# Cross-attention stage on one core: where two TensorE steps stand in the order of a unit

## The chip, the cores and the metric

The kernel runs on one core of one Trainium2 chip. A core has TensorE (PE), VectorE (DVE), ScalarE (ACT), GpSimd (POOL) and SyncE (SP, which only issues transfers here). Each engine takes its instructions in the order of its own program and they meet through semaphores. The metric is the device time of one execution in microseconds (us).

## The reference

The reference is a stack of four layers over x (4, 256, 512), each a gated cross-attention on a context (4, 64, 512) and a gated feed-forward part:

```python
x = x + jnp.tanh(g_xattn[3]) * _L3_xattn_ref(_layernorm(x, axis=-1), ctx_4096, mask, L3 weights ...)
x = x + jnp.tanh(g_ffn[3]) * _L3_ffn_ref(_layernorm(x, axis=-1), L3 ffn weights ...)
```

The change lies in the fourth cross-attention. It has 32 query heads and 8 key and value heads of width 128, an RMS norm over each query head and key head, a softmax over 64 keys, and an output projection:

```python
q = (hidden_states @ q_proj_w.T).reshape(B, Q, 32, 128).transpose(0, 2, 1, 3)
k = (cross_attention_states @ k_proj_w.T).reshape(B, KV, 8, 128).transpose(0, 2, 1, 3)
v = (cross_attention_states @ v_proj_w.T).reshape(B, KV, 8, 128).transpose(0, 2, 1, 3)
q = rmsnorm(q, q_norm_w); k = rmsnorm(jnp.repeat(k, 4, axis=1), k_norm_w); v = jnp.repeat(v, 4, axis=1)
scores = jnp.einsum('bhqd,bhkd->bhqk', q, k) * scale + attention_mask
attn = jax.nn.softmax(scores, axis=-1)
out = jnp.einsum('bhqk,bhkd->bhqd', attn, v)
return out.transpose(0, 2, 1, 3).reshape(B, Q, 4096) @ o_proj_w.T
```

## The kernel before

The program is written engine by engine; every engine's order is the order of its Python function, and waits are written by hand as semaphore counts. The fourth attention consists of `pe_x3`, `act_x3`, `dve_x3`, `pool_x3` and `sp_x3`.

It is cut into `NU0` = 32 units, u = 4 g + b. Group g (0 to 7) is one key head with its four query heads, b (0 to 3) one batch entry of 256 rows (two tiles, tt = 0 and 1). Products that need full precision are made of three (`mm3`, lines 150 to 152) from a high and a low half of each operand: ScalarE writes the high half, VectorE or POOL the rest.

The parts of a unit on TensorE:

- `queries(u, tt)`: twelve products of 512 columns, into bank tt.
- `turn_q(u, tt)`: four transposes of the queries (line 963) into bank 2.
- `scores(u)`: keys `kT` as weights against the turned queries (line 972) into bank 2. The scores come out with keys on the partitions, so ScalarE copies them to `S_TURNED` (line 1130) and `turn_s(u)` turns them back with four transposes (line 982) into bank 3.
- On VectorE `shift(u)` scales bank 3 by the queries' norm (line 1238), adds the mask (line 1242), takes the maximum (line 347) and subtracts it (line 349). ScalarE's `exps(u)` and VectorE's `norm(u)` finish the softmax.
- `turn_p(u)`: four transposes of the probabilities (line 991) into bank 4. ScalarE's `probs_t(u)` writes the high half, VectorE's `probs_low(u)` (line 1253) the low one.
- `outputs(u, tt)`: six products (lines 150 to 152) into bank 5 + tt, which VectorE's `add(u, tt)` adds to X (line 1265).

The output projection is folded into the values ahead of time, eight products a group: `fold_outputs` (line 940) into bank 7, copied by ScalarE's `folded_high` (line 1106) and subtracted by VectorE's `folded_low` (line 1258). `folds(u, slot)` says which fold stands in which of three slots of a unit. For b = 0 and 1 these are slots 1 and 2, for b = 2 slot 2 alone, for b = 3 all three; the later folds of a group are made at b = 0 and 1, the first ones of the next group at b = 2 and 3.

Once a group `keys_values(g)` makes keys and values: sixteen products of line 917 and eight of line 921, all into bank 7. ScalarE copies them (lines 1092 to 1096), VectorE squares and sums the keys (`key_squares`), POOL makes the scale (`key_scale`), VectorE applies it (`key_norm`, line 1222), and `turn_k(g)` (line 928) turns the keys on TensorE at b = 2, behind `turn_q(u + 2, 1)`. Bank 7 is one chain of ten pieces a group (`piece(r)`): each waits until ScalarE, and for a fold VectorE too, is through with the piece before.

The units are pipelined by two. The loop over u on TensorE runs: `queries(u + 2, 0)`, `turn_p(u)`, the fold of slot 0, `queries(u + 2, 1)`, `turn_q(u + 2, 0)`, the fold of slot 1, `outputs(u, 0)`, `turn_q(u + 2, 1)`, `turn_k(g + 1)` if b = 2, `outputs(u, 1)`, `scores(u + 2)`, the fold of slot 2, `turn_s(u + 2)`, and `keys_values(g + 1)` if b = 1. VectorE's loop runs: `shift(u + 1)`, `probs_low(u)`, `key_squares` if b = 2, the low half of the fold of slot 0, the sums of squares, `norm(u + 1)`, `key_norm` if b = 2, the low half of slot 1, `add(u, 0)`, `add(u, 1)`, the low half of slot 2, and in the last group row statistics (line 1346). The split weights of the next group's queries come from ScalarE (`high_q`) and POOL (`split_q`) at b = 0 and 1, two chunks of four at a time.

Of the kernel before, what the change touches and what calls it, by code (L numbers as in the profile page):

```python
# [18 lines left out]
NG, HG, DH = 8, 4, 128  # L19
# [38 lines left out]
def build(nc, x_d, ctxT_d, ctxB_d, gx_d, gf_d, wkv_d, w0q_d, w3q_d, wo_d, w4_d, sc4_d, ze4_d, l1wqv_d, l1kr_d, l1o_d,  # L58
# [3 lines left out]
    with ctx:  # L62
# [49 lines left out]
        def bank(i, n=1):  # L112
            return PS[:, i, :] if n == 1 else PS[:, i:i + n, :].rearrange("p a b -> p (a b)")
# [34 lines left out]
        def mm3(out, ah, al, bh, bl, first, last_):  # L148

            nc.tensor.matmul(out, ah, bh, start=first, stop=False)  # L150
            nc.tensor.matmul(out, ah, bl, start=False, stop=False)  # L151
            return nc.tensor.matmul(out, al, bh, start=False, stop=last_)  # L152
# [29 lines left out]
        def lows(n):  # L182
            return T * sum(k not in PLAIN for k in range(n))
# [178 lines left out]
        def s_slot(u):  # L362
            return s_sb[:, (u % 4) // 2, (u % 2) * 512:(u % 2 + 1) * 512]
# [6 lines left out]
        NU0 = NG * B  # L370
# [433 lines left out]
        def wq3(g):  # L804
            at = X3B if g % 2 == 0 else R16r[:, 12288:16384]
            return (at[:, 0:2048].rearrange("p (c n) -> p c n", c=C),
                    at[:, 2048:4096].rearrange("p (c n) -> p c n", c=C))
# [94 lines left out]
        def pe_x3(pe):  # L902
            def piece(r):
                if r:
                    if (r - 1) % PIECES3 in (0, K_AT):
                        pe.wait_ge(A3["piece_hi"], r)
                    else:
                        pe.wait_ge(A3["piece_lo"], folded(r - 1) + 1)
                return bank(7)

            def keys_values(g):
                o = piece(PIECES3 * g) if g else bank(6)
                pe.wait_ge(A3["kv_in"], 16 * (g + 1))
                for j in range(2):
                    for c in range(C):
                        at = c * 2 * DH
                        nc.tensor.matmul(o[:, j * P:(j + 1) * P], CT[:, c, j * P:(j + 1) * P], WKV3[:, at:at + DH],
                                         start=c == 0, stop=c == C - 1)
                for c in range(C):
                    at = c * 2 * DH + DH  # L920
                    i = nc.tensor.matmul(o[:, 256:512], WKV3[:, at:at + DH], CT[:, c, :], start=c == 0, stop=c == C - 1)
                i.then_inc(A3["piece_mm"], 1)
# [20 lines left out]
            def queries(u, tt):  # L943
                g, b = divmod(u, B)
                if u:
                    pe.wait_ge(A3["q_sq"], 2 * u - 1 + tt)
                if g == 0:
                    pe.wait_ge(lo_ready, lows(6) + 2 * b + tt + 1)
                tok = slice((2 * b + tt) * P, (2 * b + tt + 1) * P)
                hi, lo = wq3(g)  # L950
                for c in range(C):
                    if b == 0 and tt == 0:
                        pe.wait_ge(A3["q_split"], C * g + c + 1)
                    i = mm3(bank(tt), HTh[:, c, tok], HTl[:, c, tok], hi[:, c], lo[:, c], c == 0, c == C - 1)
                i.then_inc(A3["q_mm"], 1)
# [20 lines left out]
            def turn_s(u):  # L976
                pe.wait_ge(A3["qT_ready"], 3 * u + 3)
                if u:
                    pe.wait_ge(A3["s_read"], u)
                for h in range(HG):  # L980
                    at = (h ^ u % 2) * P
                    i = nc.tensor.transpose(bank(3)[:, at:at + P], S_TURNED[:, h * P:(h + 1) * P], ident[:])
                i.then_inc(A3["s_mm"], 1)

            def turn_p(u):
                pe.wait_ge(A3["probs"], u + 1)
                if u:
                    pe.wait_ge(A3["pt_lo"], u)
                for pr in range(2):
                    for tt in range(2):  # L990
                        i = nc.tensor.transpose(bank(4)[:, (pr * 2 + tt) * P:(pr * 2 + tt + 1) * P],
                                                s_slot(u)[:, tt * 256 + pr * P:tt * 256 + (pr + 1) * P], ident[:])
                i.then_inc(A3["t_mm"], 1)
# [43 lines left out]
            turn_q(1, 1)  # L1037
            scores(1)
            fold_outputs(0, 0, 3)
            turn_s(1)  # L1040
            for u in range(NU0):
                g, b = divmod(u, B)
                more = u + 2 < NU0
                if more:
                    queries(u + 2, 0)
                turn_p(u)
                if u == NU0 - 2:
                    pe.wait_ge(A3["q_sq"], 2 * NU0)
                    pe_turn7(pe, 0)
                    pe_turn7(pe, 1)  # L1050
                    pe_turn7(pe, 2)
                    pe_logits(pe, 0)
                    pe_logits(pe, 1)
                if u == NU0 - 1:
                    pe.wait_ge(A3["s_read"], NU0)
                    pe_turn7(pe, 3)
                    pe_turn7(pe, 4)
                    pe_logits(pe, 2)
                    pe_turn7(pe, 5)
                for f in folds(u, 0):  # L1060
                    fold_outputs(*f)
                if more:
                    queries(u + 2, 1)
                    turn_q(u + 2, 0)
                for f in folds(u, 1):
                    fold_outputs(*f)
                outputs(u, 0)
                if more:
                    turn_q(u + 2, 1)
                if b == 2 and g + 1 < NG:  # L1070
                    turn_k(g + 1)
                outputs(u, 1)
                if more:
                    scores(u + 2)
                for f in folds(u, 2):
                    fold_outputs(*f)
                if more:
                    turn_s(u + 2)
                if b == 1 and g + 1 < NG:
                    keys_values(g + 1)  # L1080

        def act_x3(act):
            def high_q(g, cs):
# [5 lines left out]
            def keys_values(g):  # L1089
                act.wait_ge(A3["piece_mm"], PIECES3 * g + 1)  # L1090
                src = bank(7 if g else 6)
                nc.scalar.copy(kvs[:], src)
                blocks = src[:, 256:256 + B * SK].rearrange("p (r o k) -> p r o k", r=B // 2, o=2)
                turned = SWAPPED.rearrange("p (r o k) -> p r o k", r=B // 2, o=2)
                nc.scalar.copy(turned[:, :, 0], blocks[:, :, 1])
                nc.scalar.copy(turned[:, :, 1], blocks[:, :, 0]).then_inc(A3["piece_hi"], 1)
# [12 lines left out]
            def query_row(u, tt):  # L1109
                act.wait_ge(A3["q_mm"], 2 * u + tt + 1)  # L1110
                nc.scalar.copy(Q_ROW[:, tt * 512:(tt + 1) * 512], bank(tt)).then_inc(A3["q_copy"], 1)  # L1111
# [20 lines left out]
            def exps(u):  # L1132
                act.wait_ge(A3["shifted"], u + 1)
                nc.scalar.activation(s_slot(u), s_slot(u), ACT.Exp).then_inc(A3["exps"], 1)

            def probs_t(u):
                act.wait_ge(A3["t_mm"], u + 1)
                nc.scalar.copy(PTh, bank(4)).then_inc(A3["pt_hi"], 1)
# [27 lines left out]
            for u in range(NU0):  # L1166
                g, b = divmod(u, B)
                more = u + 2 < NU0
                if more:
                    query_row(u + 2, 0)  # L1170
                probs_t(u)
                if u == NU0 - 2:
                    act_norm(act, 7, (0, 1, 2))
                for f in folds(u, 0):
                    folded_high(*f)
                if more:
                    query_square(u + 2, 0)
                if u + 1 < NU0:
                    exps(u + 1)
                if more:  # L1180
                    query_row(u + 2, 1)
                    query_turned(u + 2, 0)
                for f in folds(u, 1):
                    folded_high(*f)
                if more:
                    query_square(u + 2, 1)
                    query_turned(u + 2, 1)
                if b == 2 and g + 1 < NG:
                    keys(g + 1)
                if b < 2 and g + 1 < NG:  # L1190
                    high_q(g + 1, (2 * b, 2 * b + 1))
                if more:
                    scores_turned(u + 2)
                for f in folds(u, 2):
                    folded_high(*f)
                if b == 1 and g + 1 < NG:
                    keys_values(g + 1)
            act_norm(act, 7, (3, 4, 5))
            nc.scalar.preload_act_table_set("natural_log_exp_and_others")
            nc.scalar.activation(SG[:, 0:1], gate[:], ACT.Exp, scale=-1.0).then_inc(F3["gate_exp"], 1)  # L1200
# [1790 lines left out]
```

## Time and profile before

| | |
|---|---|
| time, median of 3 runs | 1486.77 us (1485.48 to 1487.81) |
| profiled execution | 1487.0 us, span 1485.3 us |
| busy TensorE | 1320.0 us, 89% of the span |
| busy VectorE | 1130.1 us, 76% |
| busy ScalarE | 750.6 us, 51% |
| busy POOL | 369.9 us, 25% |
| mean granted TensorE clock | 0.952 |

The fourth attention's loop runs from about 899 to 1366 us of the span. Engine shares are means over eight very different stages, so they say little about this one; the rows further down are of this stage. A matmul's row gives the start and the modelled end, and neighbours overlap, so distances are best taken from start to start. "PEld" rows are weight loads, which run ahead of the products. A bracket at the end of a row gives the idle time before it and what ended it. The granted clock is 1.00 at 2.4 GHz and 0.50 at 1.2 GHz.

### The profile page before, as it was taken

How to read it: one execution, taken by the hardware profiler on the slowest of the kernel's cores; microseconds unless marked ns; L12 is line 12 of the kernel's file. 1: busy time of each engine (PE TensorE's matmuls, PEld its weight loads, DVE VectorE, ACT ScalarE, POOL GpSimd, SP SyncE). 2: the span in 40 equal slices, each digit the busy share in tenths (PEclk: the TensorE clock that was granted, in tenths of full speed). 3: DMA queues.
4: the chain of work that ended last, by engine and by line, in shares of the span. 5: the costliest groups of instructions: out<-in, count | busy, mean ns of one | idle time of the engine just before them, and what ended most of it. 6: DMA issues, size and time to landing. Idle time of an engine off the chain costs nothing.

```text
span 1485.3 us, 18416 instructions
## 1 busy us (share of the span) xinstructions
PE 1320.0 (89%) x6204; PEld 947.0 (64%) x6204; DVE 1130.1 (76%) x2109; ACT 750.6 (51%) x1581; POOL 369.9 (25%) x418
## 2 busy tenths in 40 slices
PE   8999999999998989979999988999999999998104
PEld 5665566566586768647888865766667666666102
DVE  4788998898887777975555587667676686777998
ACT  4777777787524653432222246455555564553104
POOL 1112112121257541332211032122121322212620
PEclk9999999999999999969999999999999999999557
DMA  6677987798920013034213110110110101000001
GB/s 221 170 175 178 246 216 173 190 241 199 213 80 1 1 57 73 28 80 101 72 42 106 41 43 3 70 71 1 71 57 15 72 0 71 1 1 1 1 0 57
DMA packets 37911, 127.73 MB, mean 86 GB/s; under 512 B 4944, under 2 KB 10960, under 8 KB 31680
## 3 DMA queue, kind: packets, MB, share of 16 engines
q1 hardware_dynamic: 26304, 83.38, 16.0%
q0 software_dynamic: 11520, 43.26, 15.4%
q8 instruction: 46, 0.75, 0.2%
q14 instruction: 41, 0.34, 0.1%
HBM read 72.63 MB, written 10.75 MB: 56 GB/s over the span
## 4 chain that ended last, share of the span: by engine, by line
PE 53%; DVE 24%; ACT 7%; DVEq 5%; issue 4%; DMA 4%; POOL 1%; POOLq 1%; SPq 0%
PE PS L150 10%; PE PS L152 10%; PE PS L151 10%; DVE AR L676 4%; PE PS L940 4%; PE PS L972 2%; ACT s_sb L606 2%; DVE AR L2765 2%; DVE AR L2754 2%; DVE AR L2761 2%; PE PS L510 2%; DVE AR L682 2%; DMA AR<-AR 2%; DVEq L666 2%; PE PS L535 1%
## 5 line engine op out<-in xcount | busy, mean ns | idle before, releaser
L438 POOL DMA_DIRECT2D AR<-AR x76 | 74.2, 1092 | 329.2 <-DVE AR L695 126.5
L1258 DVE TENSOR_TENSOR R16r<-PS,R16r 64x512 fp32r<-64x512 f32 x128 | 88.1, 688 | 70.5 <-ACT R16r L1106 69.1
L151 PE MATMUL PS<-R16r 128*128 128x512 f32 (+1 forms) x328 | 122.2, 373 | 0.0
L510 PE MATMUL PS<-R,HT 128*128 128x256 f32 x512 | 116.5, 381 | 3.7 <-ACT R L595 3.7
L152 PE MATMUL PS<-R16r 128*128 128x512 f32 (+1 forms) x312 | 119.1, 382 | 0.0
L535 PE MATMUL PS<-R,PT 128*128 128x512 f32 x256 | 116.1, 596 | 2.8 <-DVE X L716 2.8
L510 PEld LDWEIGHTS PS<-R,HT 128*128 128x128 f32 x512 | 94.8, 190 | 16.7 <-ACT R L595 5.1
L606 ACT ACTIVATE s_sb<-PS,sm 128x64 f32<-128x64 f32 x256 | 78.2, 338 | 52.2 <-DVE sm L701 51.5
L150 PE MATMUL PS<-HTr,R16r 128*128 128x512 f32 (+1 forms) x240 | 90.2, 376 | 4.2 <-DVE R16r L190 2.7
L150 PE MATMUL PS<-R16r,HTr 128*128 128x512 f32 (+1 forms) x224 | 91.4, 408 | 0.0
L152 PE MATMUL PS<-HTr,R16r 128*128 128x512 f32 (+1 forms) x240 | 87.8, 366 | 0.0
L1106 ACT CAST R16r<-PS 64x512 fp32r<-64x512 f32 x128 | 74.5, 582 | 24.8 <-PE PS L940 24.0
L535 PEld LDWEIGHTS PS<-R,PT 128*128 128x128 f32 x256 | 47.7, 190 | 56.9 <-issue 53.6
L151 PE MATMUL PS<-R16r,HTr 128*128 128x512 f32 (+1 forms) x224 | 83.9, 375 | 0.0
L676 DVE SCALAR_TENSOR_TENSOR AR<-AR 128x2112 f32<-128x2112 bf16 x28 | 66.0, 2359 | 14.9 <-ACT AR L583 12.1
L1111 ACT COPY AR<-PS 128x512 f32<-128x512 f32 x64 | 37.5, 586 | 78.1 <-PE PS L152 77.5
L2467 DVE TENSOR_TENSOR s_sb<-PS,s_sb 128x1024 f32<-128x1024 f32 x11 | 13.5, 1225 | 82.0 <-PE PS L152 82.0
L151 PEld LDWEIGHTS PS<-R16r 128*128 128x128 f32 x328 | 63.1, 192 | 8.5
L2424 ACT CAST R16r<-PS 128x512 fp32r<-128x512 f32 x33 | 24.8, 755 | 85.7 <-PE PS L2338 85.7
L150 PE MATMUL PS<-R16r,PTr 128*128 128x512 f32 x128 | 63.8, 498 | 4.2 <-DVE PTr L1253 4.2
L152 PEld LDWEIGHTS PS<-R16r 128*128 128x128 f32 x312 | 58.6, 188 | 11.9
L482 PE MATMUL PS<-kvs,WR 128*128 128x256 f32 x256 | 60.0, 382 | 5.8 <-ACT R L595 5.8
(332 smaller groups left out, 3562.7 us busy)
## 6 DMA issues: line engine op xcount, KB each, us to landing
AR<-AR POOLq DMA_DIRECT2D x76, 528.0 KB, 6.6
OR<-in_wo SPq DMA_DIRECT2D x12, 1024.0 KB, 12.8
dequantised<-AR SPq DMA_DIRECT2D x8, 1056.0 KB, 5.5
WR<-in_w0q SPq DMA_DIRECT2D x8, 1024.0 KB, 11.7
AR<-in_w3q SPq DMA_DIRECT2D x8, 1024.0 KB, 7.1
WR<-dequantised SPq DMA_DIRECT2D x22, 256.0 KB, 2.8
AR<-in_nf SPq DMA_DIRECT2D x4, 1056.0 KB, 9.4
nf_in<-in_nf SPq DMA_DIRECT2D x4, 1056.0 KB, 11.9
```

The lines of the kernel that those rows point to most:

```text
L150: nc.tensor.matmul(out, ah, bh, start=first, stop=False)
L151: nc.tensor.matmul(out, ah, bl, start=False, stop=False)
L152: return nc.tensor.matmul(out, al, bh, start=False, stop=last_)
L438: nc.gpsimd.dma_start(nf_below(g)[:, part], what[:, part], accum_op=ALU.add, max_dma_last_dim=4 * N_NF // 2).then_inc(added, 16)
L482: i = nc.tensor.matmul(o[:, cc * 256:(cc + 1) * 256], WQ0[:, at:at + P], kvs[:, 0:B * SK], start=True, stop=True)
L510: i = nc.tensor.matmul(bank(2 + u % 2)[:, tt * 256:(tt + 1) * 256], HT0[:, c, tok], m[:, :, c * B + b, :], start=c == 0, stop=c == C - 1)
L535: i = nc.tensor.matmul(bank(5 + tt), PT[:, at:at + P], vo[:, pr, b, :], start=pr == 0, stop=pr == 1)
L606: i = nc.scalar.activation(s_slot(u)[:, cols], bank(2 + u % 2)[:, cols], ACT.Exp, bias=stat_slot(1, u)[:, j:j + 1], accum_out=stat_slot(2, ...
L676: nc.vector.scalar_tensor_tensor(nf_above, nf_far(g, NLOW + k), rise, nf_above, ALU.min, ALU.subtract if k == 1 else ALU.add).then_inc(A0[ ...
L940: nc.tensor.matmul(o, v[:, 2 * bp * SK:2 * (bp + 1) * SK], wo3(g)[:, h * D:(h + 1) * D], start=True, stop=True).then_inc(A3["piece_mm"], 1)
L1106: i = nc.scalar.copy(VOh[rows, h // 2, b, :], bank(7)[rows])
L1258: i = nc.vector.tensor_tensor(VOl[rows, h // 2, b, :], bank(7)[rows], VOh[rows, h // 2, b, :].bitcast(F32), ALU.subtract)
```

## The change

On TensorE two steps move. `turn_s` stood at the end of the iteration that made the scores, behind the fold of slot 2; now it stands in the next iteration, behind `queries(u + 2, 0)` and ahead of `turn_p(u)`. `keys_values(g + 1)` stood at the end of the iteration with b = 1; now it stands in the iteration with b = 2, also behind `queries(u + 2, 0)` and ahead of `turn_s`. On ScalarE the copies of keys and values move with it: from the end of b = 1 to b = 2, behind `query_row(u + 2, 0)` and ahead of `probs_t(u)`. The orders of VectorE, POOL and SyncE are untouched, and so are all operations and all waits.

```diff
@@ pe_x3
             scores(1)
             fold_outputs(0, 0, 3)
-            turn_s(1)
             for u in range(NU0):
                 g, b = divmod(u, B)
                 more = u + 2 < NU0
                 if more:
                     queries(u + 2, 0)
+                if b == 2 and g + 1 < NG:
+                    keys_values(g + 1)
+                if u + 1 < NU0:
+                    turn_s(u + 1)
                 turn_p(u)
...
                     scores(u + 2)
                 for f in folds(u, 2):
                     fold_outputs(*f)
-                if more:
-                    turn_s(u + 2)
-                if b == 1 and g + 1 < NG:
-                    keys_values(g + 1)
@@ act_x3
                 if more:
                     query_row(u + 2, 0)
+                if b == 2 and g + 1 < NG:
+                    keys_values(g + 1)
                 probs_t(u)
...
                 for f in folds(u, 2):
                     folded_high(*f)
-                if b == 1 and g + 1 < NG:
-                    keys_values(g + 1)
```

## Rows read from the trace of the kernel before

**Rows 1.** Busy times from 890 to 1366 us: stretch, length, PE, PEld, DVE, ACT, POOL, clock, DMA.
```profile
890.00:1366.00 476.00, 449.37 (x2099) 322.93 (x2098) 343.02 (x565) 259.45 (x500) 103.55 (x116) 0.98 0.09 34
```

**Rows 2.** List of waits, 890 to 1366 us: total us, times, longest us.
```profile
PEld PS L982 <- ACT nf_in L1130: 15.4, 31, 1.7
PE PS L917 <- DVE R16r L1258: 15.7, 7, 2.2
```

**Rows 3.** Timeline of TensorE, a plain unit: start us, duration us, engine, line, operation.
```profile
960.22 1.13 PE L940 MATMUL PS<-WR,AR 128*128 128x512 f32 x2
961.18 0.60 PE L982 MATMUL PS<-ident,nf_in 128*128 128x128 f32 x4
961.53 0.48 PE L150 MATMUL PS<-R16r,HTr 128*128 128x512 f32 x1
...
964.36 0.60 PE L991 MATMUL PS<-ident,s_sb 128*128 128x128 f32 x4
...
968.44 0.80 PE L150 MATMUL PS<-R16r,PTr 128*128 128x512 f32 x1
```

**Rows 4.** Timeline of TensorE, group boundary at full clock (last fold at b = 1).
```profile
1046.82 1.12 PE L940 MATMUL PS<-OR,AR 128*128 128x512 f32 x2
...
1050.63 2.05 PE L917 MATMUL PS<-AR,CT 128*128 128x128 f32 x16 [2.25 <-DVE R16r L1258]
...
1054.06 0.59 PE L150 MATMUL PS<-R16r,HTr 128*128 128x512 f32 x1
...
1057.02 0.60 PE L991 MATMUL PS<-ident,s_sb 128*128 128x128 f32 x4
```

**Rows 5.** Timeline of TensorE, group boundary at a lower clock, and turn of the keys.
```profile
989.99 2.86 PE L917 MATMUL PS<-AR,CT 128*128 128x128 f32 x16 [2.25 <-DVE R16r L1258]
...
998.06 0.60 PE L991 MATMUL PS<-ident,s_sb 128*128 128x128 f32 x4
...
1003.90 0.41 PE L928 MATMUL PS<-ident,kvs 128*128 128x128 f32 x2 [0.16 <-DVE kvs L1222]
```

**Rows 6.** Timeline of TensorE, a unit with b = 3.
```profile
1010.84 0.60 PE L991 MATMUL PS<-ident,s_sb 128*128 128x128 f32 x4
1011.27 1.02 PE L940 MATMUL PS<-OR,AR 128*128 128x512 f32 x2
...
1014.93 0.60 PE L963 MATMUL PS<-ident,AR 128*128 128x128 f32 x4
1015.38 1.13 PE L940 MATMUL PS<-OR,kvs 128*128 128x512 f32 x2
```

**Rows 7.** Timeline of VectorE in the units of rows 5 and 6.
```profile
999.37 0.69 DVE L1253 TENSOR_TENSOR PTr<-PS,PTr 128x512 fp32r<-128x512 f32 x1 [6.41 <-ACT PTr L1138]
...
1003.27 0.48 DVE L1222 TENSOR_SCALAR kvs<-kvs,sm 128x128 f32<-128x128 f32 x2
...
1010.43 0.69 DVE L1238 TENSOR_TENSOR s_sb<-PS,sm 128x512 f32<-128x512 f32 x1
...
1013.35 0.68 DVE L1253 TENSOR_TENSOR PTr<-PS,PTr 128x512 fp32r<-128x512 f32 x1
1013.95 1.38 DVE L1258 TENSOR_TENSOR R16r<-PS,R16r 64x512 fp32r<-64x512 f32 x2
```

**Rows 8.** Four stretches, columns as in the first group: the clock is third from last.
```profile
402.00:412.00 10.00, 8.09 (x31) 5.48 (x30) 9.67 (x15) 3.83 (x13) 1.90 (x3) 1.00 0.81 287
462.00:472.00 10.00, 6.19 (x29) 5.17 (x29) 8.44 (x10) 4.50 (x5) 6.12 (x6) 0.67 0.00 0
990.90:994.40 3.50, 3.50 (x16) 3.14 (x15) 1.92 (x3) 0.00 (x0) 0.00 (x0) 0.52 0.88 368
1050.50:1054.00 3.50, 3.37 (x23) 3.21 (x24) 2.84 (x5) 0.00 (x0) 0.00 (x0) 1.00 1.01 426
```

**Rows 9.** Timeline of TensorE in earlier stages: two idles and what ended them.
```profile
404.23 1.96 PE L535 MATMUL PS<-R,PT 128*128 128x512 f32 x4 [1.91 <-DVE X L716]
464.08 0.63 PE L268 MATMUL PS<-ident,HN 128*128 128x128 f32 x4 [2.00 <-DVE HN L206]
```

## Prediction, made before the changed kernel was run

> **What bounds the kernel now.** Start with the busy time over the stage that the diff touches: from 890 to 1366 us TensorE is busy 449 of 476 us and VectorE 343 [rows 1]. So TensorE sets the pace, but it isn't full, and the list of waits says where it stands still: 15.7 us in seven waits in front of the key and value products (line 917), which VectorE's subtraction at line 1258 ends [rows 2]. The same list has a trap. It gives 15.4 us of weight-load idle in front of the turn of the scores (line 982), 31 times 0.5 us [rows 2]. Loads run ahead of the products, so this is not TensorE's loss. That has to be read from start times in TensorE's own order, and I do that for one unit without a key step [rows 3], a group boundary at full clock [rows 4], the same boundary at a lower clock and what follows it [rows 5], and the unit after that [rows 6]. VectorE's order in the same units [rows 7] comes next, since the change alters when its work may begin. The granted clock comes last [rows 8]. ScalarE is in no chain here that a fraction of a microsecond would shift.
>
> **Frame.** Durations are of the profiled execution, 1487.0 us (span 1485.3, 1.7 around it). The median shown is 1486.77, 0.2 lower; I sum against 1487.0 and take the 0.2 off at the end. Below, K is the moment at which TensorE starts the four transposes of the turned scores in the changed kernel.
>
> **Part 1: turn_s moves behind the first query products.** It removes nothing; four transposes cost TensorE 0.35 us wherever they stand (961.18 to 961.53 [rows 3]). What it can save is the wait for ScalarE's copy of the scores. From a slot-2 fold to the transposes of the probabilities now takes 960.22 to 964.36, 4.14 us [rows 3]. A fold followed directly by twelve query products takes 1011.27 to 1014.93, 3.66 us [rows 6], and with 0.35 for the moved transposes 4.01. The saving is 0.13 us a unit, not 0.5. It applies to the 22 iterations from u = 1 to 29 in which no keys are made. Iteration 0 I count at nothing, since its transposes of the probabilities follow the first softmax, which nothing here brings forward; at u = 30 no query products are left to hide behind and the order is unchanged. 22 x 0.13 = 2.9 us.
>
> **Part 2: keys_values moves too.** It must have bank 7 back, which ScalarE and VectorE empty after the last fold. VectorE finishes late enough that line 917 starts 3.81 us after the fold (1046.82 to 1050.63 [rows 4]). Now TensorE stands idle in that time; in the changed kernel the twelve query products fill it (fold and products take 3.66 us, so at most 0.15 us of waiting is left). At full clock, fold to probabilities takes 1046.82 to 1057.02, 10.20 us: 3.81, then 3.43 of key and value products (to 1054.06), then 2.96 of queries [rows 4]. Changed: 3.81 + 3.43 + 0.35 = 7.59. Saving 2.61, seven times: 18.3 us. The cover is the query products alone. If the product for the new group had to wait for its split weights instead, it would go. ScalarE and POOL make the last of those splits beside the previous unit's scores and fold, and the third of the four chunks is asked for only after six of the new products, so I book nothing and keep it as a rival.
>
> **Part 3: the clock.** At the boundary near 990 us the same work from line 917 to the probabilities takes 8.07 us (989.99 to 998.06 [rows 5]) against 6.39 (1050.63 to 1057.02 [rows 4]). The granted clock explains it: 0.52 from 990.9 to 994.4 against 1.00 from 1050.5 to 1054 [rows 8], that is the 1.2 GHz level against the 2.4 GHz one. Before both, TensorE sat idle 2.25 us. Four of the seven boundaries are like the first, three like the second. The excess is 1.68 us; 4 x 1.68 = 6.7 us. When the 2.25 us of idling go, I expect these to go. Do the new waits of part 4 bring them back? The longest, in front of line 928, is the 0.16 us that it has now [rows 5] and 1.91 more, less what the output products ahead of it take of the wait: 1.6 to 2.1 us. A 1.91 us idle up to 404.23 left the clock at 1.00 in the ten microseconds around it, while a 2.00 us idle up to 464.08, soon followed by another, came with a mean of 0.67 [rows 8, 9]. I put the new one nearest to the first, book the full 6.7 as saved, and keep zero as the other end.
>
> By the Trainium skill, page "TensorE: Matmul & The Clock Gate", section "Why this matters for your kernels", only idle gaps of more than about 3 us between bursts cost throughput. By that rule the 2.25 us idles are innocent, the falls have another cause and would stay, and the sum would be 6.7 us smaller. The trace speaks against it: 2.25 us of idling stand right before each of the four falls.
>
> **Part 4: what becomes late.** The scores used to be turned before the query products, so VectorE did its scaling, mask, maximum and shift (lines 1238 to 349) beside them and was waiting when the probabilities came. Now the two sets of transposes stand next to each other, and in VectorE's queue the shift of unit u + 1 stands ahead of the low half of the probabilities of unit u (line 1253). That is the wait that the change adds, and behind it are queued line 1253, the key squares, the subtraction of the folds and the next softmax. The transposes take 0.60 us to their end [rows 3], and a hand-over between engines takes at least 0.05 (VectorE's subtraction ends 1015.33, TensorE starts 1015.38 [rows 6, 7]): VectorE starts at K + 0.65. From line 1238 to line 1253 it needs 2.92 us (1010.43 to 1013.35 [rows 7]): line 1253 starts at K + 3.57 and ends at K + 4.25. Four places ask for what follows:
>
> Plain units (b = 0, 1). TensorE reaches the output products 4.08 us after the probabilities' transposes start (964.36 to 968.44 [rows 3]), at K + 4.43. The low half is there at K + 4.30 to 4.40, with a hand-over of 0.05 as above or 0.15 us (1003.75 to 1003.90 [rows 5, 7]). That is no stall, by less than 0.15. I take 0; the other end is 0.3 us in each of 15 such units, 4.5 us.
>
> Key turn (b = 2). Line 1253 to the key normalisation takes 3.90 us on VectorE (999.37 to 1003.27) and 0.63 more until TensorE starts line 928 [rows 5, 7]: K + 3.57 + 3.90 + 0.63 = K + 8.10. Before, line 928 started 5.84 us after the probabilities' transposes (998.06 to 1003.90 [rows 5]), with the moved 0.35 that is K + 6.19. TensorE is 1.91 us later, seven times: -13.4 us. The output products ahead of it, which have no fold to cover them here, wait as well, but inside the same 1.91. This work was hidden in before behind the key products, and that cover is gone. Booked in full, since the chain is one in-order queue; the lower end is 0 only if my order of events is wrong.
>
> Second fold (b = 3). The fold of slot 0 occupies bank 7, and its subtraction now comes after line 1253: start K + 4.17 (0.60 later [rows 7]), end K + 5.55 (1.38), TensorE K + 5.60. TensorE is there 4.54 us after the probabilities' transposes (1010.84 to 1015.38 [rows 6]), at K + 4.89. 0.71 us, seven times: -5.0 us. In before that fold started 0.05 us after the subtraction ended, so there was no slack to use up. Ends: 0 and, with the longer hand-over of 0.15 at both places, 0.9 each, 6.4.
>
> The next softmax ends later too, but its transposes come only in the next unit, thirteen microseconds on: nothing. In the last group VectorE has row statistics (line 1346) ahead of the shift, so it comes to it late in either kernel: nothing.
>
> **Sum.** Saved 2.9 + 18.3 + 6.7 = 27.9. Lost 13.4 + 5.0 = 18.4. Net 9.5: 1487.0 - 9.5 = 1477.5, and against the median shown 1477.3. About two thirds of the gain are given back on VectorE. The stage's end carries over one to one, since the stage after it begins with its last additions.
>
> **The rivals.** (a) The clock falls stay, because the new idles cause them or because idling never did: 1477.3 + 6.7 = 1484.0. For it: the new wait, preceded by a short one, resembles the pair near 464 us; against it: the single 1.91. (b) The tenth of slack in plain units isn't there: + 4.5, 1481.8. For it: so little room; against it: both bounds of the hand-over fit. (c) VectorE does not come in the order that I laid out and the new waits are mostly absent: up to 18.4 better, 1459; with two thirds of them gone 1465. The queue speaks against it. (d) Slower than before. Place: the two new idles, in front of line 928 and of the second fold. Mechanism: each lets the clock fall to 1.2 GHz as the 2.25 us idle did. Price: 1.68 us each, 14 places, 23.5 us, so 1501; from the eighth fall on it is slower than before by more than can be missed (12.4 us are needed to pass 1489.7). For it: four falls behind 2.25 us idles; against it: the 1.91 us idle without one, and 0.71 is far shorter. (e) The move doesn't do what it says: the query products of the new group wait for split weights, and the idle moves from line 917 to them. For it: nothing else stands between; against it: the six products of cover. 1 us a group would give 1484, the whole 2.25 us 1493.
>
> **How the numbers follow.** A measurement of this kernel can tell about 0.2%, 3.0 us, from no change: faster is below 1483.8, slower above 1489.7. The forecast, 1472 to 1481.3: 0.50, faster. (a) 0.16, of which 0.07 come out faster and 0.09 the same. (b) 0.10, faster. (c) 0.07, faster. (d) 0.09, slower. (e) 0.04, the same. What is unnamed: 0.04, half the same and half slower. Faster 0.74, same 0.15, slower 0.11. For eight in ten the range takes in the forecast, (a), (b) and a part of (c): 1469 to 1486. The predicted time is the forecast's, 1477.3.
>
> **What would show it right or wrong.** Right: the 15.7 us in front of line 917 gone to about 1 us; no stretch of lower clock at the seven boundaries; line 928 with a wait of about 1.6 to 2.1 us, seven times, ended by VectorE's kvs; line 940 at slot 1 of b = 3 starting about 5.6 us after line 982; a plain unit 12.85 us long instead of 12.98; VectorE's line 1238 with a wait ended by line 982. Wrong: waits for the low half (line 1253) in front of line 150 in every unit (b), low-clock stretches after line 928 (a, d), a wait in front of the first query product of a group (e), or line 928 without one (c).

## The result, and the profile after

The changed kernel takes 1479.68 us (median of 5, 1478.31 to 1481.97) against 1487.81 for the kernel before on the same chip (median of 5, 1485.48 to 1489.23). The ratio is 0.995, 95% interval 0.9935 to 0.9966: 0.5% faster, clear of the 0.2% that count as no change, and 2.4 us above the 1477.3 that was predicted, inside the range. The profiled execution took 1481.9 us, span 1480.2, which is 5.1 us less than the profiled execution before.

First the length of the stage, from the score product of unit 1 (line 972) to that of unit 31, in the timeline of TensorE. Before:

```profile
895.78 1.08 PE L972 MATMUL PS<-AR,kT 128*64 128x512 f32 x4 [1.54 <-ACT AR L1126]
...
1344.09 1.08 PE L972 MATMUL PS<-AR,kT 128*64 128x512 f32 x4
```

After:

```profile
897.27 1.08 PE L972 MATMUL PS<-AR,kT 128*64 128x512 f32 x4 [1.54 <-ACT AR L1125]
...
1339.21 1.08 PE L972 MATMUL PS<-AR,kT 128*64 128x512 f32 x4
```

448.31 us became 441.94: 6.4 us saved where the change acts. The medians give 8.1 us for the whole kernel, with an interval of 5.1 to 9.7, so the 6.4 lie inside it. The stage begins 1.5 us later than before. About that much comes from a fall of the clock to the lower level near 452 us, in a stage that the change does not touch, where the trace of before has none. The view of stretches for 448 to 458 us, changed kernel (the third number from the right is the granted clock; it was 1.00 before):

```profile
448.00:458.00 10.00, 9.20 (x64) 8.96 (x64) 7.03 (x15) 2.43 (x5) 7.30 (x13) 0.83 0.00 0
```

The list of waits of the changed kernel, 890 to 1366 us (total us, times, longest):

```profile
DVE s_sb L1237 <- PE PS L982: 43.0, 28, 4.3
...
PE PS L928 <- DVE kvs L1221: 11.8, 7, 1.7
...
PE PS L940 <- DVE R16r L1257: 4.1, 8, 0.8
...
PEld PS L917 <- DVE R16r L1257: 2.4, 7, 0.4
```

Below line 1078 every line number is now one or so lower. The 15.7 us in front of line 917 [rows 2] are gone, but for 2.4 us of weight-load idle. In their place stand 11.8 us in front of the turn of the keys (line 928) and most of 4.1 us in front of a fold (line 940). VectorE now waits 28 times for the turned scores.

The timeline of TensorE in a plain unit, changed kernel:

```profile
963.77 0.60 PE L982 MATMUL PS<-ident,nf_in 128*128 128x128 f32 x4
...
973.03 1.12 PE L940 MATMUL PS<-WR,AR 128*128 128x512 f32 x2
...
976.75 0.60 PE L982 MATMUL PS<-ident,nf_in 128*128 128x128 f32 x4
977.18 0.60 PE L991 MATMUL PS<-ident,s_sb 128*128 128x128 f32 x4
...
981.27 0.79 PE L150 MATMUL PS<-R16r,PTr 128*128 128x512 f32 x1
```

The unit lasts 12.98 us (963.77 to 976.75), as before. Fold to the transposes of the probabilities is 4.15 us (973.03 to 977.18), against 4.14 [rows 3]. The turned scores cost 0.43 us here, not 0.35.

The same timeline at a group boundary (b = 2), then at b = 3:

```profile
986.01 1.13 PE L940 MATMUL PS<-WR,AR 128*128 128x512 f32 x2
...
989.82 2.05 PE L917 MATMUL PS<-AR,CT 128*128 128x128 f32 x16
...
993.44 0.60 PE L982 MATMUL PS<-ident,nf_in 128*128 128x128 f32 x4
993.88 0.60 PE L991 MATMUL PS<-ident,s_sb 128*128 128x128 f32 x4
...
997.10 0.60 PE L963 MATMUL PS<-ident,AR 128*128 128x128 f32 x4
997.73 0.50 PE L150 MATMUL PS<-R16r,PTr 128*128 128x512 f32 x1
...
1001.51 0.41 PE L928 MATMUL PS<-ident,kvs 128*128 128x128 f32 x2 [1.68 <-DVE kvs L1221]
...
1008.02 0.60 PE L982 MATMUL PS<-ident,nf_in 128*128 128x128 f32 x4
1008.45 0.60 PE L991 MATMUL PS<-ident,s_sb 128*128 128x128 f32 x4
...
1013.61 1.13 PE L940 MATMUL PS<-OR,kvs 128*128 128x512 f32 x2 [0.46 <-DVE R16r L1257]
```

And VectorE beside it:

```profile
994.08 0.69 DVE L1237 TENSOR_TENSOR s_sb<-PS,sm 128x512 f32<-128x512 f32 x1 [4.31 <-PE PS L982]
...
997.00 0.68 DVE L1252 TENSOR_TENSOR PTr<-PS,PTr 128x512 fp32r<-128x512 f32 x1
...
1000.89 0.47 DVE L1221 TENSOR_SCALAR kvs<-kvs,sm 128x128 f32<-128x128 f32 x2
```

What to see: the keys' products follow the queries with no idle on TensorE (fold to line 917 is 3.81 us as in [rows 4], but now full of work). VectorE sat idle for 4.31 us while this went on, because its next instruction, line 1237, waits for the turn of the scores. From there it needs 7.28 us to the end of the key norm (994.08 to 1001.36), plus 0.15 us to hand over, and TensorE stands at line 928 until then. A small part of the delay falls earlier: the first output product starts 0.63 us after the transposes in front of it (997.10 to 997.73), 0.05 us after VectorE's low half ends (line 1252, 997.68).

The clock at the seven boundaries, view of stretches, changed kernel (two of the seven; all read 1.00, where four of seven read 0.83 before), and between them the stretch around line 928 of the boundary above, whose new wait is not followed by a lower clock either (1.00 at all seven):

```profile
929.00:939.00 10.00, 9.94 (x59) 8.24 (x57) 4.87 (x8) 3.78 (x9) 1.53 (x1) 1.00 0.70 264
...
1001.00:1011.00 10.00, 9.49 (x42) 6.39 (x43) 5.85 (x11) 4.43 (x8) 1.84 (x2) 1.00 0.00 0
...
1283.00:1293.00 10.00, 9.96 (x58) 8.28 (x57) 5.22 (x9) 3.78 (x10) 1.09 (x1) 1.00 0.01 2
```

### The profile page after: what moved, and what is told of

Read it like the earlier page. It is cut to its first block, busy times and chain, and to the rows that moved or that the text cites. A ratio compares the mean times of both kernels' runs of the same rounds, so it can differ in the third digit from the quotient of the medians.

```text
span 1480.2 us, 18416 instructions
## 1 busy us (share of the span) xinstructions
PE 1315.5 (89%) x6204; PEld 943.5 (64%) x6204; DVE 1128.0 (76%) x2109; ACT 749.6 (51%) x1581; POOL 369.4 (25%) x418
## 4 chain that ended last, share of the span: by engine, by line
PE 50%; DVE 25%; ACT 6%; DVEq 6%; DMA 5%; issue 4%; POOL 1%; POOLq 1%; SPq 0%
PE PS L150 10%; PE PS L152 10%; PE PS L151 10%; DVE AR L676 4%; PE PS L940 4%; DMA AR<-AR 3%; ACT s_sb L606 2%; PE PS L972 2%; DVE AR L2764 2%; DMA nf_in<-in_nf 2%; DVE AR L2753 2%; DVE AR L2760 2%; DVEq L666 1%; PE PS L535 1%; PE PS L510 1%
## 5 line engine op out<-in xcount | busy, mean ns | idle before, releaser
L150 PE MATMUL PS<-R16r,HTr 128*128 128x512 f32 (+1 forms) x224 | 96.1, 429 | 0.0
L151 PE MATMUL PS<-R16r,HTr 128*128 128x512 f32 (+1 forms) x224 | 84.1, 375 | 0.0
L676 DVE SCALAR_TENSOR_TENSOR AR<-OT,AR 128x2112 f32<-128x2112 bf16 x24 | 56.6, 2359 | 11.1 <-ACT OT L583 9.0
## 6 DMA issues: line engine op xcount, KB each, us to landing
WR<-in_w0q SPq DMA_DIRECT2D x8, 1024.0 KB, 11.7
```

The source lines that it names most:

```text
L676: nc.vector.scalar_tensor_tensor(nf_above, nf_far(g, NLOW + k), rise, nf_above, ALU.min, ALU.subtract if k == 1 else ALU.add).then_inc(A0[ ...
```

## The experiments

All ratios below are to the kernel before on the same chip.

**One half of the change alone: keys_values moved, turn_s left where it was.**

```diff
-                if u + 1 < NU0:
-                    turn_s(u + 1)
                 turn_p(u)
...
                     fold_outputs(*f)
+                if more:
+                    turn_s(u + 2)
```

(This diff is against the changed kernel; `turn_s(1)` is also back in front of the loop.)

> The changed kernel with turn_s back at the end of the iteration, so that keys_values alone has moved. Theory A (all that the change loses comes from turn_s standing next to turn_p; keys_values alone brings the gain): the wait in front of line 928 falls from 1.68 us to 0.2 to 0.7 (the copies of keys and values now stand ahead of the probabilities' copy on ScalarE), the second fold of b = 3 doesn't wait, no clock falls at the boundaries. 2.5 us a boundary and 6.7 us of clock, less up to 3.5: 1464 to 1468. Theory B (the new waits come from keys and values being made in the unit that turns them): the wait in front of line 928 stays at 1.5 us or more, and the time is 1475 or above.

Measured: 1464.89 us against 1486.73, ratio 0.9859 (0.9832 to 0.9887). The timeline of TensorE at the same boundary:

```profile
982.39 1.95 PE L917 MATMUL PS<-AR,CT 128*128 128x128 f32 x16
...
985.90 0.60 PE L991 MATMUL PS<-ident,s_sb 128*128 128x128 f32 x4
...
992.07 0.41 PE L928 MATMUL PS<-ident,kvs 128*128 128x128 f32 x2 [0.49 <-DVE kvs L1222]
```

Line 928 starts 6.17 us after the probabilities' transposes, where it took 7.63 in the changed kernel and 5.84 before [rows 5]. The fold of b = 3 has no wait in the list. No boundary shows the lower clock. So theory A holds: this half brings 1.4%, and the other half takes about two thirds of it away (of 22 us the changed kernel keeps 8).

**The other half alone: turn_s moved, keys_values left.**

```diff
                     queries(u + 2, 0)
+                if u + 1 < NU0:
+                    turn_s(u + 1)
                 turn_p(u)
...
-                if more:
-                    turn_s(u + 2)
```

> The kernel before with turn_s alone moved behind the first query products; keys_values stays at the end of b = 1. Theory A: nothing is saved, a plain unit stays 12.98 us, line 928 waits about 1.7 us and the second fold of b = 3 about 0.5, seven times each (16 to 17 us), the idle in front of line 917 grows by the 0.4 us of the transposes that stood in it (3 us), and the clock falls stay at four or more boundaries: 1504 to 1512. Theory B: no wait at line 928, 1485 to 1490.

Measured: 1511.2 us, ratio 1.0162 (1.0134 to 1.019). TensorE at a boundary near the one above, and the list of waits:

```profile
989.60 2.05 PE L917 MATMUL PS<-AR,CT 128*128 128x128 f32 x16 [2.68 <-DVE R16r L1257]
...
1004.10 0.41 PE L928 MATMUL PS<-ident,kvs 128*128 128x128 f32 x2 [1.67 <-DVE kvs L1221]
```

```profile
PE PS L917 <- DVE R16r L1257: 18.8, 7, 2.7
...
PE PS L928 <- DVE kvs L1221: 11.7, 7, 1.7
PE PS L940 <- DVE R16r L1257: 4.1, 8, 0.8
```

The 11.7 and 4.1 us are those of the changed kernel, so they come with turn_s and not with the keys. A plain unit took 12.97 us (963.56 to 976.53): turn_s gains nothing by its move. The idle in front of the keys grew from 2.25 to 2.68 us, and five of the seven boundaries now show the lower clock, two of them for longer than before (0.72 over 12 us):

```profile
1050.00:1061.00 11.00, 9.53 (x47) 8.42 (x48) 2.13 (x4) 1.91 (x5) 0.97 (x1) 0.84 0.57 228
1111.00:1123.00 12.00, 9.32 (x34) 7.59 (x35) 1.84 (x3) 2.67 (x6) 3.10 (x4) 0.72 0.53 182
```

The two halves do not add up to the whole by their times (-21.8 and +24.5 us give +2.7, the whole is -8.1). Most of the 10.8 us between them can be named. At full clock, last fold to the transposes of the probabilities takes 10.20 us before, 7.70 with the keys moved, 10.64 with turn_s moved and 7.87 with both, where adding the two changes gives 8.14: 7 x 0.27 = 1.9 us. turn_s alone brings more of the lower clock, which can't occur when the keys have moved as well (two of its five falls last about twice as long, so they weigh as seven against four before, 3 x 1.68 = 5.0 us). And the 7 x 0.33 = 2.3 us by which line 928 comes later when the keys alone move lie inside the longer delay of the changed kernel. That makes 9.2 us, an estimate from these rows.

**The price of the clock by itself: the wait filled with work.** The kernel before, with nine products nobody reads in front of the wait.

```diff
             def keys_values(g):
+                for _ in range(9 if g else 0):
+                    nc.tensor.matmul(bank(4), HTh[:, 0, 0:P], HTl[:, 0, 0:512], start=True, stop=True)
                 o = piece(PIECES3 * g) if g else bank(6)
```

> The kernel before with nine products of 512 columns, whose result nobody reads, put into bank 4 in front of the wait of keys_values at each of the seven boundaries, so that TensorE is busy through most of its 2.25 us of idling but wins no time by it. If the idling causes the clock falls (theory A): none of the four falls at line 917, the keys' products take the short time at all seven boundaries, and the kernel is 6 to 7 us faster than before, about 1481. If the falls have another cause (the rule of an idle of about 3 us, or a fixed rhythm): they stay, and the time is within 1 us of before.

Measured: 1480.22 us against 1486.73, ratio 0.9956 (0.9939 to 0.9972), 6.5 us faster for 63 more products. The filler (line 913) ends where the wait ended, the boundary itself is no shorter, but the clock is 1.00 at all seven (one is shown):

```profile
927.26 2.33 PE L913 MATMUL PS<-R16r,HTr 128*128 128x512 f32 x9
929.76 2.05 PE L919 MATMUL PS<-AR,CT 128*128 128x128 f32 x16 [0.16 <-DVE R16r L1260]
```

```profile
927.00:938.00 11.00, 10.84 (x61) 9.09 (x60) 4.72 (x7) 3.77 (x9) 2.12 (x3) 1.00 0.69 240
```

The idling causes the falls, and they cost the 6.7 us that the prediction booked: from the first to the seventh key product the profile shows 353.28 us (929.76 to 1283.04) against 359.96 before (929.56 to 1289.52). The rule of the Trainium skill ("TensorE: Matmul & The Clock Gate", "Why this matters for your kernels"), which asks only for idle gaps of no more than about 3 us, would have left them in place; here the measurement decides against it.

**Is VectorE's queue the chain? One link taken out.** In both kernels the addition of the mask is left out of `shift` (the mask holds zeros).

```diff
-                nc.vector.tensor_tensor(s4, s4, mask_sb.rearrange("p (t k) -> p t k", t=2).unsqueeze(2)
-                                        .to_broadcast([P, 2, HG, SK]), ALU.add)
-                dve.drain()
```

> The changed kernel without the addition of the mask (its 692 ns on VectorE and the drain behind it, 0.76 us of every shift; the mask holds zeros here). If VectorE's queue from the turned scores to the key norm is the chain that sets line 928 and the second fold (theory A), line 928 waits 0.76 us less and the second fold not at all, 5.3 + 4.3 = 9.6 us over seven groups: 1468 to 1472. If another engine's step ends those waits, less than 2 us.

> The kernel before without the addition of the mask (zeros here), the control for the run on the changed kernel. There the shift lies beside the query and key products: 0 to 2 us (the last unit's softmax is in the chain once, 0.8 us, and the first once): 1485 to 1488.

Measured: the changed kernel without it takes 1470.4 us against 1483.75, ratio 0.9916 (0.99 to 0.9933); the kernel before without it 1482.04, ratio 0.9974 (0.9958 to 0.9991). The changed kernel's stage, TensorE at a boundary and the next unit:

```profile
1106.04 0.60 PE L982 MATMUL PS<-ident,nf_in 128*128 128x128 f32 x4
1106.48 0.60 PE L991 MATMUL PS<-ident,s_sb 128*128 128x128 f32 x4
...
1109.72 0.60 PE L963 MATMUL PS<-ident,AR 128*128 128x128 f32 x4
1110.07 0.48 PE L150 MATMUL PS<-R16r,PTr 128*128 128x512 f32 x1
...
1113.35 0.41 PE L928 MATMUL PS<-ident,kvs 128*128 128x128 f32 x2 [1.19 <-DVE kvs L1221]
```

And its list of waits, 890 to 1366 us:

```profile
PE PS L928 <- DVE kvs L1221: 8.9, 7, 1.5
```

Line 928 starts 7.31 us after line 982 instead of 8.07: 0.76 less, exactly the link, at six of the seven boundaries (0.43 less at the other). The wait in front of it is only 0.49 us shorter (1.68 to 1.19, in all 11.8 to 8.9 us, where 5.3 less were expected), because the rest is won at the output products ahead of it, which no longer wait for the low half (0.35 us from 1109.72 to 1110.07, against 0.63). The fold of b = 3 no longer appears among the waits.

From the first to the seventh key product the stage takes 344.96 us (929.90 to 1274.86) against 353.57 (931.02 to 1284.59), 8.6 us less, 1.4 us a group. The control, the kernel before without the addition, takes 357.57 there against 359.96:

```profile
930.29 2.98 PE L917 MATMUL PS<-AR,CT 128*128 128x128 f32 x16 [2.25 <-DVE R16r L1255]
...
1287.86 2.05 PE L917 MATMUL PS<-AR,CT 128*128 128x128 f32 x16 [2.25 <-DVE R16r L1255]
```

Of its 2.4 us, 1.7 are one boundary less at the lower clock (three, not four). So the link is worth 8.6 us where turn_s has moved and under one where it hasn't.

The times of the whole kernel say less. The 1470.4 us lie in the expected 1468 to 1472, but the kernel before ran 3 to 4 us faster in this series than in the others. By the ratios, 0.9916 against the changed kernel's 0.995, the gain is about 5 us, not 9.6. The control gained 3.9 us by the medians where at most 2 were expected: its last softmax is 0.8 us shorter, the missing fall of the clock is 1.7, and what is left lies within its interval (1.3 to 6.2 us). The difference of the two gains is about 1 us by the ratios and about 4 by the means of the runs, with an uncertainty of about 4, against 6.2 us (8.6 less 2.4) in the profiles. So the distances in the profiles carry this verdict, and the times leave open how much of the 8.6 us reaches the end of the kernel.

**A version that takes the good half and trims it.** As keys_moved_only, with ScalarE's copy of the probabilities ahead of the copies of keys and values.

```diff
+                probs_t(u)
                 if b == 2 and g + 1 < NG:
                     keys_values(g + 1)
-                probs_t(u)
```

> As keys_moved_only, and on ScalarE the copy of the probabilities stands ahead of the copies of keys and values. The low half then starts about 0.5 us earlier, but the key squares about 0.3 us later than before: the wait in front of line 928 is 0.2 to 0.5 us. Theory A: 0 to 2 us faster than keys_moved_only, 1463 to 1467. Theory B: no difference to it, and both above 1475.

Measured: 1463.78 us, ratio 0.9848 (0.9823 to 0.9873). The wait in front of line 928 is 0.33 us at the same boundary, 2.5 us in all against 3.7. The intervals of this and of keys_moved_only overlap, so the trim itself is not resolved by the times. The profiles show 1.0 us over six groups (339.31 us from the first to the seventh key product against 340.26). Both are clearly faster than the kernel before and than the changed one.

## Why the prediction was right, point by point

| term | predicted, us | from the trace, us |
|---|---|---|
| turn_s behind the queries, plain units | 22 x 0.13 = 2.9 | 0 (4.15 against 4.14) |
| keys behind the queries | 7 x 2.61 = 18.3 | 7 x 2.33 = 16.3 (10.20 to 7.87) |
| clock at the boundaries | 4 x 1.68 = 6.7 | 6.7 (no fall left; 6.5 with the wait filled) |
| turn of the keys waits | 7 x 1.91 = 13.4 | 7 x 1.79 = 12.5 (7.63 against 5.84) |
| second fold waits | 7 x 0.71 = 5.0 | 7 x 0.62 = 4.3 (5.16 against 4.54) |
| net | 9.5 | 6.2 (6.4 between the ends of the stage) |

The mechanism of every large term was right, and so was its place. The sum came closer than its terms: 4.9 us too much were booked as saved and 1.6 too much as lost, and the two errors partly cancel. That the medians give 8.1 us and not 6.2 is owed to no term. Single falls of the clock outside this stage come and go between runs (one near 452 us here, none there in the kernel before), and the interval is wide enough for both. VectorE's side was right almost to the hundredth: line 1237 starts at K + 0.64 (0.65 predicted), line 1252 at K + 3.56 (3.57), line 928 at K + 8.07 (8.10), the fold at K + 5.59 (5.60).

**The term that failed is part 1**, 2.9 us that did not exist. Its step was "four transposes cost TensorE 0.35 us wherever they stand", taken from the shown start of line 982 to the shown start of the product behind it. But in these timelines the shown start of the first product behind transposes runs ahead of its work: the product after it comes 0.32 us later, where products otherwise follow each other at 0.23. The two rows behind the 961.53 of [rows 3], kernel before:

```profile
961.85 0.40 PE L151 MATMUL PS<-R16r,HTr 128*128 128x512 f32 x1
962.08 0.39 PE L152 MATMUL PS<-R16r 128*128 128x512 f32 x1
```

The transposes cost 0.43 to 0.44 us, as seen where transposes follow transposes (976.75 to 977.18). With 0.44 the comparison 3.66 + 0.44 = 4.10 against 4.14 leaves nearly nothing, and 0.06 more went into the hand-over from the products. The move of turn_s took nothing off the unit: the list of waits gave 0.5 us for ScalarE's copy and I gave 0.13, and a plain unit is as long as before (12.98 us).

The same error is in part 2: 0.09 us for the transposes, and 0.19 for the keys' products (989.82 to 993.44 is 3.62, where I had 3.43 to the shown start of a query product, again a start that runs ahead). The row behind the 1054.06 of [rows 4] comes 0.43 us later, not 0.23:

```profile
1054.49 0.40 PE L151 MATMUL PS<-R16r,HTr 128*128 128x512 f32 x1
```

In part 4 it worked the other way: TensorE came to line 928 and to the fold 0.09 us later than I thought and so waited that much less.

**Part 3** rested on one reading, that an idle of 1.6 to 2.1 us is nearer to the 1.91 us that left the clock alone than to the pair near 464 us. The new idles are 1.67 to 1.69 us, seven times, and none is followed by a fall. With turn_s alone moved the same wait stands there seven times, again without one. This decided the sign: the products and the waits cancel (16.3 against 16.8), and by these terms the whole gain of the changed kernel is the clock's. From the first to the seventh key product it takes as long as the kernel before with its idling filled (353.57 and 353.28 us). One argument of this part was weak: 2.25 us of idling stood right before each of the four falls, but also before the three boundaries without one. Only the run with the wait filled shows that the idling is what the falls need.

**Plain units**: the low half (line 1252) is ready at 980.98 and TensorE shows its product at 981.27, with 0.24 us of weight-load idle in front of it and the same length of unit. There is no stall, and the 0.29 us between the two, hand-over included, is a little more than was predicted (K + 4.25 to K + 4.43).

```profile
980.30 0.68 DVE L1252 TENSOR_TENSOR PTr<-PS,PTr 128x512 fp32r<-128x512 f32 x1
```

**The rivals.** (a) and (d), falls of the clock behind the new idles: none was seen. (b), stalls in plain units: none, though the slack is thin. (c), the waits mostly absent: no, they cost 16.8 us. (e), waits for split weights: no wait stands in front of the first query product of a group. The measured median lies 2.4 us above the forecast, of which part 1's missing 2.9 is the largest piece.

## What to carry to other kernels

Before moving a step behind other work to hide its wait, ask which engine lives on that step's result: here TensorE's transposes were cheap to leave early and fed a VectorE chain of seven microseconds, which the earlier place hid at no cost. Judge each half of a combined move by itself; one half was worth 1.4% and the other cost about two thirds of that. And a short idle on TensorE is to be priced with the clock that it may cost behind it, which can be read from the same products at either level.

## What the runs showed of the hardware

- How often an idle of TensorE was followed by the 1.2 GHz level. In front of the keys' products: 0.16 to 0.20 us, 0 of 7 (wait filled); 2.25 us, 4 of 7 (before) and 3 of 7 (before without the mask addition); 2.68 us, 5 of 7, two of them about twice as long as the others (turn_moved_only). In front of line 928, with other work around it: 1.67 us, 0 of 7 (changed kernel) and 0 of 7 (turn_moved_only). Behind the same idle at the same place the clock falls in some groups and not in others.
- Filling an idle with products that nobody reads made the kernel 0.44% faster (1480.22 us against 1486.73).
- Both kernels without the mask addition show, at one of the seven boundaries only, 0.40 us between the start of the last key-square instruction and the next instruction on VectorE (999.83 to 1000.23 in the control), where it is 0.07 to 0.08 elsewhere, and nothing in the trace explains it. Line 928 waits 0.3 us longer there. Its cause stays open.
